# GpSimd adds the keys' parts into the masked copies; projection, outputs and turns in another order of TensorE

## The reference

```
Q = (decoder_input @ W_q).reshape(B, Sd, HEADS, HEAD_DIM)
K = (encoder_output @ W_k).reshape(B, Se, HEADS, HEAD_DIM)
V = (encoder_output @ W_v).reshape(B, Se, HEADS, HEAD_DIM)
scores = jnp.einsum('bqhd,bkhd->bhqk', Q, K) / jnp.sqrt(jnp.float32(HEAD_DIM))
attn = jax.nn.softmax(scores, axis=-1)
out = jnp.einsum('bhqk,bkhd->bqhd', attn, V).reshape(B, Sd, E)
return out @ W_o + b_o
```

## Time and profile before

| what | value |
|---|---|
| time, median of 3 runs (lowest, highest) | 213.25 us (212.55, 214.83) |
| the profiled execution: its own time | 213.41 us |
| its span, first to last instruction | 211.6 us |
| mean granted TensorE clock over the span | 0.969 |

### The profile page before, as it was taken

The page is one execution under the profiler, slowest core; times in us unless marked ns, Lnnn a source line. Parts: engine busy times, 40 slices in busy tenths (PEclk is TensorE's granted clock), DMA queues, the critical chain, the costliest instruction groups (busy, mean ns, idle before and its releaser), DMA issues.

```text
span 211.6 us, 4097 instructions
## 1 busy us (share of the span) xinstructions
PE 181.0 (86%) x1300; PEld 139.4 (66%) x1300; DVE 154.5 (73%) x437; ACT 116.8 (55%) x229; POOL 58.5 (28%) x85
## 2 busy tenths in 40 slices
PE   5699799899999999999999678789999999888231
PEld 4389498678799888889899355546555666445110
DVE  2889758667468565654767996799899999965684
ACT  2257467742322222443354289977989797858242
POOL 3714274691000000300220164333223232304400
PEclk9999999999999999999999999999999999999755
DMA  6999300000000000000000000000000000000002
GB/s 221 378 417 377 137 0 2 0 3 0 0 0 5 0 0 3 0 0 0 3 0 0 2 0 5 0 5 0 2 3 0 0 0 0 0 3 0 0 2 99
DMA packets 4225, 8.81 MB, mean 42 GB/s; under 512 B 880, under 2 KB 1904, under 8 KB 3952
## 3 DMA queue, kind: packets, MB, share of 16 engines
q1 hardware_dynamic: 2480, 7.60, 9.3%
q10 hardware_dynamic: 1728, 1.00, 1.6%
HBM read 5.98 MB, written 0.52 MB: 31 GB/s over the span
## 4 chain that ended last, share of the span: by engine, by line
PE 58%; DVE 19%; issue 9%; ACT 8%; POOL 2%; DMA 2%; DVEq 1%; ACTq 0%; POOLq 0%
PE banks L1176 12%; PE bank L1010 7%; PE bank L1012 7%; PE bank L1011 7%; DVE negm L860 6%; PE bank L1207 5%; PE bank L1241 4%; ACT rest L468 2%; PE banks L1012 2%; PE banks L1011 2%; PE banks L1010 2%; DVE stats L610 2%; PE bank L1250 2%; ACT raw L493 2%; DMA xs<-in_x 2%
## 5 line engine op out<-in xcount | busy, mean ns | idle before, releaser
L860 DVE TENSOR_REDUCE negm<-bank 128x2 f32<-128x512 f32 x64 | 42.0, 687 | 2.4 <-PE bank L1207 1.5
L435 ACT ACTIVATE att<-bank 128x512 f32<-128x512 f32 x32 | 19.2, 599 | 38.4 <-PE bank L1012 25.7
L300 POOL TENSOR_TENSOR keyed<-rest,const 32x256 fp32r<-32x256 f32 x32 | 19.5, 608 | 61.2 <-DVE rest L850 49.9
L493 ACT ACTIVATE raw<-banks 128x1024 f32<-128x1024 f32 x32 | 32.5, 1023 | 3.5 <-PE banks L1226 3.2
L1207 PE MATMUL bank<-keyed 128*128 128x512 f32 x64 | 25.9, 447 | 4.1 <-DVE negm L860 1.8
L815 DVE SCALAR_TENSOR_TENSOR xs<-banks,rw,xs 128x128 f32<-128x128 f32 x64 | 18.0, 344 | 5.9 <-PE banks L1176 5.8
L1176 PEld LDWEIGHTS banks<-raw,attT 128*128 128x128 f32 x176 | 21.3, 192 | 0.8
L1176 PE MATMUL banks<-raw,attT 128*128 128x128 f32 x176 | 21.4, 275 | 0.0
L1010 PE MATMUL bank<-xT,w 128*128 128x512 f32 x48 | 19.9, 416 | 1.4 <-DVE xT L744 1.4
L1207 PEld LDWEIGHTS bank<-keyed 128*128 128x128 f32 x64 | 10.7, 188 | 12.7 <-issue 9.4
L1011 PE MATMUL bank<-xT,w 128*128 128x512 f32 x48 | 18.8, 391 | 0.0
(11 more groups left out here) (201 smaller groups left out, 390.2 us busy)
## 6 DMA issues: line engine op xcount, KB each, us to landing
raw<-in_w SPq DMA_DIRECT2D x1, 2048.0 KB, 10.7
keyed<-negm SPq DMA_DIRECT2D x1, 2048.0 KB, 8.8
raw<-in_w SPq DMA_DIRECT2D x1, 1024.0 KB, 9.8
xs<-in_x SPq DMA_DIRECT2D x2, 256.0 KB, 3.4
ctxT<-in_ctxT SPq DMA_DIRECT2D x1, 512.0 KB, 4.6
ctx<-in_ctx SPq DMA_DIRECT2D x1, 512.0 KB, 6.5
wl<-in_wl SPq DMA_DIRECT2D x1, 256.0 KB, 6.8
wqkraw<-in_wq ACTq DMA_DIRECT2D x1, 256.0 KB, 7.1
```

The source lines that it names most:

```text
L300: pool.tensor_tensor(km[rows, g, j, :], ks[rows, g % 2, :], const[rows, C_ZERO:C_ZERO + 1].broadcast_to([QUAD, SEQ]), ALU.add)\
L435: act.activation(silus[:, k, :], bk[2 * k][:, :], ACT.Silu).then_inc(S["silu_s"], 1)
L493: act.activation(probs[:, slot, 2 * r:2 * r + 2, :, :].rearrange("p h k q -> p (h k q)"), pair[r][:, :], ACT.Exp, scale=ATT_SCALE).then_in ...
L860: dve.tensor_reduce(negm[:, g % 2, r // 2, c0:c0 + QUAD + 1:QUAD], bk[1 + r % 2][:, :].rearrange("p (h k) -> p h k", h=2), AX.X, ALU.max, ...
```

## The change

- GpSimd makes all four masked copies, each as the sum of two whole tensors: `kraw`, the keys as they came from the projection (a new copy by ScalarE), and `hiK`, now the rounded keys times a column of signs. `stack_keys` and ScalarE's masked copies are gone. `hiK` has two buffers.
- The six projection matmuls stand together directly behind the shifted scores and ahead of score piece 3. ScalarE rounds between its two exponentials, as before.
- The outputs of groups 0 to 12 are formed in two halves of two heads, with score piece 1 between them.
- Score pieces alternate between banks 1 and 2 by group, and the transposes of the maxima with them.
- The turns of outputs, the output layer and the turns of the norm stand behind piece 3 and mostly one group later or earlier than before; piece 0 of the group after next comes last. The loops are written out for all 16 groups.

```diff
-            def masked_keys(m, g, first):
-                pool.wait_ge(S["ks_s"], m + 1)
-                if not first:
-                    pool.wait_ge(S["s2_ps"], 2 * (m - 3))
-                for j in range(2, HPG):
+            def masked_keys(m):
+                pool.wait_ge(S["k_hi"], m + 1)
+                pool.wait_ge(S["k_raw"], m + 1)
+                if m >= G:
+                    pool.wait_ge(S["s2_ps"], 2 * (m - G + 1))
+                for j in range(HPG):
                     rows = slice(QUAD * j, QUAD * (j + 1))
-                    pool.tensor_tensor(km[rows, g, j, :], ks[rows, g % 2, :],
-                                       const[rows, C_ZERO:C_ZERO + 1].broadcast_to([QUAD, SEQ]), ALU.add)\
-                        .then_inc(S["km_pool"], 1)
-                    pool.wait_ge(S["km_pool"], 2 * m + j - 1)
+                    pool.tensor_tensor(km[rows, m % G, j, :], kraw[rows, m % 2, :], hiK[rows, m % 2, :], ALU.add)\
+                        .then_inc(S["km_s"], 1)
+                    pool.wait_ge(S["km_s"], HPG * m + j + 1)
...
             def proj_hi(m, bank=0):
                 act.wait_ge(S["proj_ps"], m + 1)
...
+                act.wait_ge(S["qs_s"], m)
+                act.copy(hiQ.bitcast(r32), bk[bank][:, 0:SEQ]).then_inc(S["q_hi"], 1)
+                if m >= 2:
+                    act.wait_ge(S["km_s"], HPG * (m - 1))
+                act.activation(hiK[:, m % 2, :].bitcast(r32), bk[bank][:, SEQ:2 * SEQ], ACT.Identity,
+                               scale=const[:, C_AK:C_AK + 1], bias=const[:, C_ONE:C_ONE + 1]).then_inc(S["k_hi"], 1)
+                act.copy(kraw[:, m % 2, :], bk[bank][:, SEQ:2 * SEQ]).then_inc(S["k_raw"], 1)
...
+        def score_bank(m, r):
+            if m == 0:
+                return 2 - r % 2
+            return 2 - m % 2 if r == 2 else 1 + m % 2
...
+            def dve_group(m):
+                b, g = m // G, m % G
+                more = m + 1 < GROUPS
+                if more:
+                    maxima(m + 1, 0)
+                shifted(m)
+                if more:
+                    maxima(m + 1, 1)
+                if m + 2 < GROUPS:
+                    stack_queries(m + 2)
+                if more:
+                    maxima(m + 1, 2)
+                if m == 0:
+                    sum_moments(1)
+                if m in (2, 3):
+                    later_norm_lo(g)
+                if g == 0 and b >= 2:
+                    add_attention(b - 2, slice(TPB * (b - 2), TPB * (b - 1)))
+                if b > 0 and g == 1:
+                    normalise(b - 1, 0)
+                if 0 < b < BATCH - 1 and g == 2:
+                    normalise(b - 1, 1)
+                if more:
+                    maxima(m + 1, 3)
...
+            def pe_group(m):
+                b, g = m // G, m % G
+                more, final = m + 1 < GROUPS, m == GROUPS - 1
+                turn_maxima(m)
+                bank7_free(m)
+                if m >= 2:
+                    outputs(m - 2, LOW, 0 if final else 7)
+                if more:
+                    scores(m + 1, 1)
+                if m >= 2 and not final:
+                    outputs(m - 2, HIGH)
+                if more:
+                    scores(m + 1, 2)
+                shifted_scores(m)
+                if m + 3 < GROUPS:
+                    project(m + 3)
...
+                if more:
+                    scores(m + 1, 3)
+                if m in (2, 3):
+                    pe.wait_ge(S["o_ev"], m - 1)
...
+                if g == 0 and b >= 2:
+                    output_layer(b - 2)
+                if b >= 1 and g == 1:
+                    turn_outputs(b - 1, 0 if b < BATCH - 1 else 1)
+                if 1 <= b < BATCH - 1 and g == 2:
+                    turn_outputs(b - 1, 1)
+                if m in TURNED_AT:
+                    turn_normalised(b - 1)
...
+                if m + 2 < GROUPS:
+                    scores(m + 2, 0)
```

More of the change, by code:

```diff
@@ L311, in add_bias @@
                 pool.wait_ge(S["bo_added"], h + 1)
[L313 to L322, removed]
             pool.wait_ge(S["ctx_lo"], 1)
@@ L327, in _ @@
             for m in range(2):
-                masked_keys(m, m, True)
+                masked_keys(m)
             values(0, True)
[L330 to L333, removed]
+            for m in range(GROUPS):
+                b, g = m // G, m % G
+                if g == 1 and b > 0:
+                    values(b, False)
+                if m + 2 < GROUPS:
+                    masked_keys(m + 2)
+                if m == 0:
+                    deviation_and_shift(1)
+                if m in (G, G + 2):
+                    add_bias((m - G) // 2)
             inverse_deviation(4, 0, CHUNKS[0])
@@ L471, in proj_hi @@
             def proj_hi(m, bank=0):
                 act.wait_ge(S["proj_ps"], m + 1)
[L473 to L484, removed]
@@ L494, in exps, with o_copy @@
                                ACT.Exp, scale=ATT_SCALE).then_inc(S["p_s"], 1)
-            def o_copy(m, g, bank=7):
+            def o_copy(m, bank=7):
                 act.wait_ge(S["pv_ps"], m + 1)
[L499 to L521, removed]
@@ new lines, in o_copy, with turned_out, act_group @@
+                if m >= G and m % G == 1:
+                    act.wait_ge(S["oT_ps"], TPB * (m // G))
+                act.copy(heads_out[:, m % (G + 1), :], bk[bank][:, SEQ:2 * SEQ]).then_inc(S["o_ev"], 1)
+            def turned_out(b):
+                act.wait_ge(S["aoT_ps"], b + 1)
+                act.copy(aoT[:, :], bk[7][:, 0:SEQ]).then_inc(S["aoT_ev"], 1)
+            def act_group(m):
+                b, g = m // G, m % G
+                if 2 <= m < GROUPS - 1:
+                    o_copy(m - 2)
+                exps(m, 0)
+                if m in (2, 3):
+                    later_norm_hi(g)
+                if m in TURNED_AT:
+                    turned_out(b - 1)
+                if m + 3 < GROUPS:
+                    proj_hi(m + 3)
+                exps(m, 1)
+                if m in (1, 2):
+                    for t in range(TPB * (g + 1), TPB * (g + 2)):
+                        third_scaled(t)
@@ L545, in _ @@
             proj_hi(2)
[L546 to L549, removed]
+            for m in range(GROUPS):
+                act_group(m)
             def chunk_norm(c):
@@ L1338, in _ @@
                 if n >= UNITS - 2:
-                    for a in range(2):
-                        project(n - UNITS + 2, n - UNITS + 2, 0, a, bank=7)
+                    project(n - UNITS + 2, 7)
                 up(n)
```

305 lines of the change are left out of this document (120 added, 185 removed).

## The result

The changed kernel takes 233.4 us (median of 4 runs, 233.12 to 233.96) beside 213.8 for the kernel before on the same chip: 1.092 times the time, 95% interval [1.0856, 1.0991]. The forecast was 233, 9% slower.

What follows compares the result with a forecast made beforehand. PE's order to piece 3 and VectorE's work were taken to bound the stage together. Groups of 4.9 + 4.6 + 11 x 5.56 + 8.0 + 5.5 + 4.8 = 89.0 us against 69.4 add 19.6 to 213.4: 233 us, range 220 to 239.

Steps and rivals of the forecast that it cites:

- What bounds the kernel: Attention stage: PE's order to piece 3, 4.23 us, plus 1.33 us behind it; 5.56 us a plain group against 4.00.
- Outputs in two halves: PE, groups 2 to 14: each half takes 0.99 us; outputs with pieces 1 and 2 go from 1.69 to 2.64 us.
- Work behind piece 3 that VectorE awaits: Groups 2, 3, 5, 6, 8, 9, 10, 12: turns or output layer delay the last maximum, about 1.0 us each, + 8.0 us.
- Plain groups: Stage groups where VectorE awaits nothing that PE issues behind piece 3; forecast at 5.56 us each.
- The other groups: Groups 0, 1, 13 and 14, with differing work: forecast at 4.9, 4.6, 5.5 and 4.8 us.
- Copies of the keys: GpSimd's four additions, 2.6 to 5.2 us a group, covered by one group of lead: price 0.
- Half price: Rival, PE's outputs: half the heads take half the time, 0.51 us instead of 0.99; 220.5 us, chance 0.08.
- VectorE relieved: Rival, attention stage: VectorE sets the pace and losing `stack_keys` saves 6.6 us; 206.8 us, chance 0.04.
- GpSimd late: Rival, five groups: additions of 1.3 us make keys late, 6.5 us more, 239.5 us; chance 0.08 for over 239.

Runs made afterwards that it cites:

- all three together: Changed kernel with outputs whole again, score piece 3 ahead of the projection, and VectorE's maximum 3 ahead of normalise, addition and norm: 213.0 us, ratio 0.997.

## Why the prediction was right, by its own steps

*What bounds the kernel.* PE's order up to piece 3 plus 1.33 us behind it: held. The group after is 4.46 us to piece 3 and 1.18 behind it, 5.64, for 4.23 + 1.33 = 5.56. Behind piece 3 the maximum started 0.44 us later (165.04 to 165.48), not 0.54; ahead of it the outputs with both pieces took 160.95 to 163.79, 2.84, not 2.64. A piece of scores between calls of another kind holds PE for 0.43 us (161.94 to 162.37), and I had taken half of a pair, 0.33.

*Outputs in two halves.* Held, 0.99 each where the clock was at 1.00. In the kernel before, the halves alone cost 12.1 us of stage; taken out of the changed kernel they gave back 8.5 of its 20.6, less because the wait for the queries then showed.

*Work behind piece 3 that VectorE awaits.* Held: + 1.0 in eight groups was the price. Plain groups took 5.64, seven of the eight 6.42 to 6.60, that is + 0.8 to + 0.95, and maximum 3 put first gave back 0.87 in each.

*Group 2*, the eighth, took 7.25, not 6.56. Windows of the changed kernel there:

```profile
119.00:123.00 4.00, 2.67 (x18) 1.68 (x18) 3.68 (x15) 2.13 (x5) 2.23 (x5) 1.00 0.00 0
123.00:127.00 4.00, 3.24 (x20) 2.25 (x20) 2.71 (x6) 2.21 (x3) 3.59 (x6) 0.87 0.01 2
127.00:128.50 1.50, 1.14 (x4) 0.29 (x2) 1.29 (x2) 1.50 (x4) 1.17 (x3) 0.50 0.00 0
128.50:130.00 1.50, 1.50 (x10) 0.59 (x9) 0.42 (x1) 1.03 (x3) 1.34 (x3) 0.70 0.05 11
```

The granted clock fell to 0.50, that is 1.2 GHz, late in the second window, at about 126.0 in group 1, and came back in the fourth, at about 129.4 in group 2. PE had been busy for 2.67 of 4 us in the first window and for 3.24 in the second, and had waited for VectorE between. The first half of the outputs took 1.40 us there. The second half, at 1.00 again, took 0.99. The prediction had named this risk and not priced it: it cost 0.41 in that half and 0.24 ahead of it, where the outputs started 0.61 instead of 0.37 us after `turn_maxima`. Group 1 paid too: it took 4.79 us, and 4.32 in the kernel with maximum 3 put first, which has the same order there and kept the clock at 1.00. Together that is 1.1 us. In the kernel before, the clock stayed at 1.00 through the same groups. But with outputs whole and with half again of GpSimd's additions it fell in group 0 (5.24 and 5.26 us instead of 4.63) and was at 1.00 again in groups 1 and 2, and PE's order is the same in group 0 of all three. So where it falls is in part a matter of the single execution, and one trace of each kernel does not show what the change has to do with it.

*The other groups.* 4.62, 4.79, 5.59 and 5.06 for 4.9, 4.6, 5.5 and 4.8. The sum: 89.0 predicted, 90.0 measured, and the difference is 0.25 in the plain groups, 0.55 in the eight (group 2 gives 0.69, the rest - 0.14), 0.26 in the others. Without the fall of the clock it would be 88.9, an estimate (90.0 - 1.1). That it comes so near is in part luck: a plain group is 0.23 longer up to piece 3 and 0.15 shorter behind it, and group 1 is 0.28 shorter than its 4.6. That the profiled execution came out at 233.5 and not at 234 us is luck too, for its head was 0.6 shorter.

*Copies of the keys.* Price 0: nobody in the stage waits for GpSimd, and with half again of the additions one group of fifteen does clearly. The cover is the group of lead: where piece 0 stood ahead of the projection, PE did wait. An addition took 0.72 us, inside my bounds of 0.65 and 1.3 and near the lower.

*The rivals.* Half price falls by the halves alone. VectorE relieved falls: it waits 22.5 us, and one instruction more is worth 1.0 us even where it waits little (5.4 us between 125 and 195 us). GpSimd late falls.

What the prediction did not see cost it nothing, but misled two of my later expectations, for the outputs whole and for all three together: the projection's wait for the queries, and that VectorE's wait for piece 1 was filled before by the queries and by the very instruction that was taken away.

## What to carry to other kernels

When an instruction list of one engine is reordered, go through the reader of every moved result on the other engines and move it too: here three orders of a few lines each cost 20 us, and with them put right and the queries moved as well the kernel is 1.4% faster than before. Don't split a call whose parts run side by side in column strips without looking at what a half costs: here it cost as much as the whole. And an engine's instruction that fills a wait is worth little when taken away (1.0 us here, for an instruction of 0.47 us in every group); look first at what the engine waits for behind it.

## What the runs showed of the hardware

Two heads' outputs in two column strips take 0.99 to 1.00 us, four heads in four strips 1.03, in the groups shown of three kernels, at a granted clock of 1.00; at 0.50, coming back to 1.00 within the call, two heads took 1.40. GpSimd's addition of two whole 32 x 256 tensors takes 0.72 us on average (64 of them), where the one with a column as second operand took 0.61 (32), with the same output. ScalarE's scaled copy out of the bank, here from the list of its instructions in the stage of before and then of after, became slower when it got a column as scale beside the column as bias, and another output tile; which of the two did it was not tried:

```profile
L468 ACT ACTIVATE rest<-bank,const 128x256 fp32r<-128x256 f32 x13 | 6.2, 475 | 0.3
```

```profile
L470 ACT ACTIVATE w<-bank,const 128x256 fp32r<-128x256 f32 x13 | 7.5, 577 | 0.0
```
